# Layer 1 of a two-layer GNN kernel: the table product moves to the end of TensorE's step

## The reference

```python
edge_index = jnp.stack([src, dst])
h = jnp.maximum(_layernorm(x, axis=-1), 0.0)
x = x + _L0_gnn_ref(h, edge_index, edge_weight)          # segment_sum(h[src] * e, dst)
h = jnp.maximum(_layernorm(x, axis=-1), 0.0)
x = x + _L1_gnn_ref(h, edge_index, edge_attr_4, edge_attr_32, ...)
...
# _L1_gnn_ref: an MLP makes 4 x 8 x 8 weights for every edge, these mix the source's features
h = jax.nn.relu(edge_feat @ W1 + b1)
w = (h @ W2 + b2).reshape(e, 4, MUL, MUL)
m0 = ALPHA * (einsum('ei,eio->eo', s_e * sh0, w_000) + C110 * einsum('eim,em,eio->eo', v_e, sh1, w_110))
m1 = ALPHA * (einsum('ei,em,eio->eom', s_e, sh1, w_011) + einsum('eim,eio->eom', v_e * sh0, w_101))
out0 = segment_sum(m0, dst); out1 = segment_sum(m1, dst)   # and a product with si_w0, si_w1 per node
```

## Time and profile before

| | |
|---|---|
| median of 3 timed runs | 6261.46 us (6260.98 to 6275.74) |
| the profiled execution | 6323.1 us, its span 6321.3 us |
| mean granted TensorE clock | 0.991; 1.00 from 3500 to 6200 us |
| layer 0, first table product | 66.03 us |
| layer 1, first gather to last message | 2946.3 to 6283.3 us |
| busy share of the span | PE 98%, DVE 88%, POOL 75%, ACT 58% |
| a step of layer 1 | about 6.35 us, 522 steps, 516 with a table product |

### The profile page before, as it was taken

How to read it: one execution, slowest core, us unless ns; L and a number is a source line. 1 busy time by engine, 2 the same in 40 slices (tenths; PEclk the granted TensorE clock), 3 DMA queues, 4 the chain that set the end, 5 groups by cost and what they waited for, 6 DMA issues and landing times.

```text
span 6321.3 us, 162006 instructions
## 1 busy us (share of the span) xinstructions
PE 6163.8 (98%) x44113; PEld 5028.0 (80%) x44113; DVE 5586.9 (88%) x13297; ACT 3639.9 (58%) x14243; POOL 4715.7 (75%) x4985
## 2 busy tenths in 40 slices
PE   5999999999999999996999999999999999999998
PEld 5888888888888888885777777777777777777776
DVE  7888887787777778776999999999999999999997
ACT  2222222222222222225888888888888888888887
POOL 4777777777777777776777777777777777777776
PEclk9999999999999999997999999999999999999998
DMA  4111111111111111111111111111111111111111
GB/s 110 34 33 33 34 34 34 34 33 32 34 34 32 34 34 34 32 34 39 43 40 40 42 40 41 40 42 40 40 42 40 41 40 42 40 40 42 40 41 35
DMA packets 290428, 247.44 MB, mean 39 GB/s; under 512 B 105235, under 2 KB 286867, under 8 KB 289927
## 3 DMA queue, kind: packets, MB, share of 16 engines
q1 hardware_dynamic: 133500, 163.65, 9.6%
q0 software_dynamic: 156096, 80.23, 8.9%
q10 hardware_dynamic: 802, 3.22, 0.2%
HBM read 241.49 MB, written 5.25 MB: 39 GB/s over the span
## 4 chain that ended last, share of the span: by engine, by line
PE 64%; POOL 24%; issue 9%; DVE 1%; DMA 1%; POOLq 1%; ACT 0%; ACTq 0%; DVEq 0%; SPq 0%
PE hp_ps L875 25%; POOL z L467 24%; PE w_ps L723 12%; PE w_ps L804 11%; PE sc_ps L828 5%; PE w_ps L801 3%; PE w_ps L793 3%; PE sc_ps L831 2%; PE sc_ps L836 1%; PE w_ps L734 1%; PE hp_ps L734 0%; DMA z<-h_table,idx 0%; DMA x_sb<-in_x 0%; POOLq L464 0%; DMA span_table<-span_i 0%
## 5 line engine op out<-in xcount | busy, mean ns | idle before, releaser
L467 POOL DMA_INDIRECT z<-h_table,idx x4878 | 4671.6, 958 | 1531.3 <-issue 1454.3
L723 PE MATMUL w_ps<-parts,pick 128*128 128x448 f32 x12180 | 2562.3, 369 | 69.8 <-DVE pick L1039 66.0
L723 PEld LDWEIGHTS w_ps<-parts,pick 128*128 128x128 f32 x12180 | 2268.3, 188 | 279.9 <-issue 75.7
L569 ACT ACTIVATE z<-z,squares 128x32 f32<-128x32 f32 x3132 | 726.7, 309 | 2064.4 <-DMA z<-h_table,idx 1952.3
L875 PE MATMUL hp_ps<-parts,pick 128*128 128x448 f32 x7224 | 1610.6, 373 | 0.0
L875 PEld LDWEIGHTS hp_ps<-parts,pick 128*128 128x128 f32 x7224 | 1315.9, 188 | 269.9 <-issue 145.4
L1039 DVE TENSOR_TENSOR pick<-sc_ps,feat 128x896 fp32r<-128x896 f32 x870 | 911.4, 1081 | 3.4 <-PE w_ps L723 3.4
L804 PE MATMUL w_ps<-w_sb,squares 64*128 64x256 f32 x6264 | 872.9, 378 | 0.0
L804 PEld LDWEIGHTS w_ps<-w_sb,squares 64*128 64x128 f32 x6264 | 746.0, 188 | 66.9 <-issue 0.5
L1202 DVE TENSOR_TENSOR prod<-w_ps,squares 128x384 f32<-128x384 f32 (+1 forms) x1044 | 780.4, 747 | 0.6 <-ACT squares L626 0.6
L626 ACT ACTIVATE squares<-z,squares 128x32 f32<-128x32 f32 x3132 | 713.7, 307 | 0.0
(11 more groups left out here) (93 smaller groups left out, 5375.9 us busy)
## 6 DMA issues: line engine op xcount, KB each, us to landing
z<-h_table,idx POOLq DMA_INDIRECT x4878, 2.4
feat<-key_table SPq DMA_DIRECT2D x346, 192.0 KB
squares<-in_ft_sh SPq DMA_DIRECT2D x261, 216.0 KB
feat<-key_table SPq DMA_DIRECT2D x174, 128.0 KB
h_table<-big SPq DMA_DIRECT2D x10, 280.0 KB
rel_sb<-in_dst_t SPq DMA_DIRECT2D x1, 1566.0 KB, 8.3
idx_all<-in_src_t SPq DMA_DIRECT2D x1, 1530.0 KB, 10.5
squares<-in_ew_t SPq DMA_DIRECT2D x1, 1530.0 KB, 14.2
```

Source lines behind the costliest of these rows:

```text
L467: pool.indirect_dma_start(z[:, r, u, :], None, rows, bass.IndirectOffsetOnAxis(ap=idx[:, r, u:u + 1], axis=0)).then_inc(z_in[r], 16)
L569: last = nc.scalar.activation(z[:, r, u, :], z[:, r, u, :], ACT.Copy, scale=ew_all[:, bass.ds(n * G + u, 1)])
L723: mm = pe.matmul(fold_ps[:, pick_banks[k], 0:NC * D], pick[:, k, blk, :], parts[:, t, :, blk, :], start=(blk == 0 and t == 0), stop=(blk = ...
```

## The change

In TensorE's step of layer 1, the fold and the window sums with their waits go up in front of the table product. No instruction is added or removed, and the lists of the other engines are the same. The table product's line is 887 in the new file.

```diff
                     weights(n, q, q).then_inc(wts_ready, 1)
 
+                if s is None or s >= 3:
+                    pe.wait_ge(sum1_reduced, n - 2)
+                    if s is None or s >= 4:
+                        pe.wait_ge(acc1_done, n - 3)
+                    fold_sums((r - 3) % 2).then_inc(sum1_folded, 1)
+
+                if s is None or 2 <= s <= S + 1:
+                    v = (r - 2) % R1
+                    pe.wait_ge(msg1_ready, n - 1)
+                    pe.wait_ge(hot1_ready, n - 1)
+                    window_sums(v, v % 3).then_inc(sum1_ready, 1)
+
                 bt, t = before(b, r, R1, -2)
                 if s is None or R1 <= s + 2 < S:
...
                     mm.then_inc(picked1, 1)
-
-                if s is None or s >= 3:
-                    pe.wait_ge(sum1_reduced, n - 2)
...
-                    window_sums(v, v % 3).then_inc(sum1_ready, 1)
             supertiles(pe, R1, edge_layer, lag=3, written_out=1)
```

## The result

| | median | runs |
|---|---|---|
| before | 6261.22 us | 6257.82 to 6275.74 |
| changed | 6347.74 us | 6347.43 to 6351.64 |

The ratio is 1.0136, 95% interval 1.0122 to 1.0149: the change costs 86.5 us. The changed kernel's profiled execution took 6347.9 us, as long as its timed runs. The one of the kernel before, on which the prediction rests, took 6323.1 us, 62 us over its median, so the two traces can't simply be subtracted.

The account below looks back on a forecast made before the run. POOL's gathers were taken as the bound, 12.71 us per pair, TensorE and VectorE close behind. The ring's 6.62 + 6.25 = 12.87 us adds 41 us on 258 pairs: 6302, or 6335 by another reading; forecast 6310 us, range 6258 to 6355.

Parts of the forecast that it names:

- the ring: Layer 1, even steps: table product, VectorE's selection to reduction, fold, next product close a loop of 6.62 us; chance 0.62.
- first link: From the table product's end to VectorE's line 1255: taken as 0.14 us, bounds 0.05 and 0.23 us.
- The odd step: TensorE's step without `pick` on VectorE: reduction in time, no wait, 6.24 us, taken as 6.25 in the pair.
- the kernel before's pair: Even plus odd step in layer 1 before the change: 12.71 us, set by POOL's ten gathers, one of them longer.
- pair after less pair before: Layer 1 loss per pair of steps: 12.87 against 12.71 us, 0.16 us more, on 258 pairs 41 us.
- From the profiled execution to the median: Whole kernel: profiled execution 61.6 us over the median; spread evenly on all, the changed median becomes 6302 us.
- The second reading: The 61.6 us lie on the gathers: POOL's pair 0.13 us shorter in timed runs, loss 33 us larger, 6335 us.
- The cover: The table product covered the fold's wait for the reduction by 3.5 us before; the change leaves 0.5 us of slack.
- Fewer long gathers: Rival: VectorE's two-SBUF-operand lines no longer meet gathers, at most 52 us faster, down to 6210 us; chance 0.05.
- the same time: Rival: ring at its low end, pair 12.69 us, below POOL's 12.71, so POOL still bounds at 6262 us; chance 0.24.
- More long gathers: Rival: two gathers per pair each 0.3 us longer, pair 13.1 us, 103 us slower, 6365 us; chance 0.09.
- my own test: If ScalarE still waits for gathers at 4000 us and POOL's gathers have no pause, POOL is still the bound.

Follow-up runs that it names:

- e7: Changed kernel with four gathers per step in layer 1 in place of five, one tile computed from stale rows: 6353.83 us, one run.
- e2: Changed kernel with VectorE summing the selected groups (line 1262, 0.52 us) ahead of the reduction of the window sums: 6490.15 us, ratio 1.0351.
- e4: Changed kernel with VectorE taking the sums and the new pick ahead of the wait for the table product, then selecting and reducing: 6269.55 us, ratio 0.9999.
- e1: Kernel before, unchanged, run and profiled a second time: 6271.27 us, ratio 1.0001; profiled execution 6261.8 us.
- e3: Kernel before with VectorE summing the selected groups ahead of the reduction of the window sums: 6269.42 us, ratio 0.9994.
- e9: Changed kernel with lines 1187 and 1231 multiplying by a constant, so each reads one SBUF operand in place of two: 6352.52 us, one run.
- e8: Kernel before with VectorE's line 1240 reading its row numbers from SBUF in place of PSUM, so both inputs are in SBUF: 6271.73 us, one run.
- e5: Kernel before with the fold alone moved ahead of the table product, the window sums staying behind it: 6336.95 us, ratio 1.0103.

## Why the prediction was right, and where it was off

The time, 6347.74 us, lies in the range of 6258 to 6355, the sign was right, and so was the mechanism of the loss, the ring. The forecast of 6310 was 38 us too low, and that the range still held the time is in part luck: its upper end was 6335 with 23 us for a first link of 0.23 us, and that link measured 0.14.

- *The ring.* 6.62 us predicted, 6.61 measured (3998.71 to 4005.32). By links: product to line 1255 0.14, as taken; line 1255 to the reduction's end 2.19 against 2.20; to the fold 0.13 against 0.06; fold to product 1.05 against 1.12. The last two differ because in that pair the weights came later than the reduction; in e7, where the fold does wait, they are 0.06 and 1.11. The odd step came out at 6.2 to 6.3 against 6.24. That the ring is the cause is shown by e2 (longer), e4 (opened) and e7 (gathers out of the way).
- *The step that failed: the kernel before's pair.* I took 12.71 us from the one profiled execution and called POOL, with a stretched gather per pair, the bound. (Even there 165 gathers over 1.0 us fall on 212 pairs, so it was not one in each.) Typical is 12.48 us (e1), where TensorE and POOL are level. The term "pair after less pair before" was 12.87 - 12.71 = 0.16 us; measured it is 12.83 - 12.48 = 0.35, times 258 90 us. The after side was right to 0.04 us, the before side off by 0.23.
- *From the profiled execution to the median.* The 61.6 us between them were spread over two readings, evenly or on the gathers, and I leaned to the first. Neither is what happened: profiling costs no time here (6261.8 us in e1, 6347.9 changed). The second reading, 6335, was nearer only because it made the kernel before's pair shorter.
- *The cover.* The slack of the fold in the kernel before is there: a delay of 0.52 us in e3 costs nothing. In the changed kernel the same delay costs 142 us (6490.15 - 6347.74).
- *The rivals.* Fewer long gathers and the same time fell with the result. More long gathers: the stretch did grow, from 0.2 to 0.35 us per pair, and it is just the difference between the ring and ten gathers; with most of it gone (e9) the time stays. It was an effect of the ring, not a price beside it.
- *What was to be seen.* Line 1255's wait, the steps of 6.6 and 6.2 us and the fold once per pair were as said. Wrong was that POOL would stand still and ScalarE's waits for gathers go, and with it that ScalarE needed no look: TensorE waits for its relu 154 times, 34.7 us, and takes there a part of the delay that was forecast for the fold alone. By my own test ("wrong, if ScalarE still waits") POOL would have been the bound; e7 and e9 show that it wasn't. POOL was held at the ring's pace through the stretched gather, and a profile can't tell that from a bound.
- *The Trainium skill* ("SBUF — State Buffer", section "Who interferes with whom") has a tensor_tensor with two SBUF inputs contend with GpSimd's reads; the gather of 1.49 us in e8 agrees with that. It infers that descriptor writing isn't held up by such an instruction. For these indirect gathers as a whole that doesn't come out: they took 0.94 us when nothing met them, 1.49 us in e8 and up to 1.346 us at lines 1231 and 1187 in the changed kernel.

## What to carry to other kernels

When a step is moved in front of another on one engine, look at what its waits were covered by, and follow the engine that releases them: if that engine now first waits for the step that was moved behind, a ring closes, and its length is the sum of the links on both engines. The consumer must take results in the order in which the producer makes them; here e4 restores the time by moving one selection on VectorE behind the sums and the pick. And where the profiled execution is 1% off the median of the timed runs, a second profile of the unchanged kernel comes before any sum.

## What the hardware showed

- A gather that starts while VectorE runs an instruction with two SBUF operands takes longer than its 0.94 us: 1.49 us where 0.67 us of the instruction were left (e8), up to 1.346 us at lines 1231 and 1187 (0.29 us each) in the changed kernel. With one operand in PSUM none of 212 took over 0.962 us.
- Only the start of a gather is open to this. In the first execution of the kernel before, 3500 to 6200 us, the 147 gathers that start between 0.05 us ahead of line 1231 and its end take 1.062 to 1.387 us; the 268 that were under way for 0.06 us or more when it began take 0.957 at most. This ties GpSimd to VectorE's step: in the changed kernel one gather in each of 210 pairs is stretched, and GpSimd, which would else run ahead, shows no pause. The edge isn't the same at every instruction: in e8 a gather that starts 0.05 us ahead of line 1240 isn't held (4006.37 against 4006.42 us). Why is open.
- In e9, instructions with one SBUF operand in place of lines 1231 and 1187 left gathers of up to 1.146 us, also unexplained.
- Of two equal programs with three engines level at 12.5 us for a pair, one execution ran at 12.71 us throughout and one at 12.48. What starts the slower pattern wasn't found; the timed runs of the kernel before show a few values above the rest (6300.46 us among runs near 6271, 6313.81 among runs near 6263), but no run here shows whether these had the same pattern.
- A matmul with 32 columns of its own in front of one of 448 costs TensorE 0.18 us from start to start (e5), and 0.02 in front of other 32-column matmuls (changed kernel).
